# Eight fused transformer and Mamba batches on one core: stack reload in four transfers per table, LoRA rows on one partition, maxima over two key tiles, masks on diagonal columns

## What is computed

```python
x = _layernorm(x + _L0_attn_ref(x, ...), axis=-1)   # two causal attentions, 16 heads of width 8
x = _layernorm(x + _L0_ffn_ref(x, ...), axis=-1)    # FP4-quantized gated FFN, inner width 352
x = _layernorm(x + _L1_attn_ref(x, ...), axis=-1)   # Mamba block: 256 channels, 16 states, scan over time
x = _layernorm(x + _L1_ffn_ref(x, ...), axis=-1)    # FFN of width 512 with token-made low-rank weights
```

## Time and profile before

| | |
|---|---|
| runs, device us | 1017.21 median, 1008.09 to 1023.85 |
| profiled execution, device us | 1005.87 |
| its span, first to last instruction, us | 1003.6 |
| PE / VectorE / ScalarE / GpSimd busy | 692.3 / 724.7 / 461.2 / 153.4 us |
| mean granted TensorE clock | 0.849 of 2.4 GHz |
| DMA moved | 65.93 MB, 66 GB/s |

### The profile page before, as it was taken

One profiled execution on the slowest core, in us unless ns is written; L12 is line 12 of the kernel. 1 busy time (PEld: TensorE's weight loads), 2 busy tenths in 40 slices (PEclk: granted clock), 3 DMA queues, 4 the chain that ended last, 5 costly groups with the idle time before them and its releaser, 6 DMA issues.

```text
span 1003.6 us, 12436 instructions
## 1 busy us (share of the span) xinstructions
PE 692.3 (69%) x4131; PEld 407.2 (41%) x4131; DVE 724.7 (72%) x1295; ACT 461.2 (46%) x931; POOL 153.4 (15%) x265
## 2 busy tenths in 40 slices
PE   3247665786679776877778667956795777855555
PEld 1124344344544444434533454434543453433122
DVE  2716156986789687968897788868896779863951
ACT  2213432662566246634556356625662256436312
POOL 5512013013110412002300230022100000000000
PEclk9997867797889889889979897989898798976775
DMA  4421501361035303350136103520353013002300
GB/s 120 78 54 40 100 1 38 108 139 24 11 99 138 68 0 107 103 103 0 43 120 126 24 11 118 136 48 10 97 133 67 1 47 115 22 0 70 104 0 5
DMA packets 41151, 65.93 MB, mean 66 GB/s; under 512 B 8113, under 2 KB 30338, under 8 KB 38786
## 3 DMA queue, kind: packets, MB, share of 16 engines
q1 hardware_dynamic: 38946, 64.51, 26.0%
q10 hardware_dynamic: 2176, 1.05, 0.6%
HBM read 57.68 MB, written 7.86 MB: 65 GB/s over the span
## 4 chain that ended last, share of the span: by engine, by line
PE 37%; DVE 33%; DMA 11%; ACT 8%; issue 8%; SPq 1%; POOL 0%; DVEq 0%; ACTq 0%
PE ps_s L1052 9%; PE ps_f L1052 8%; DVE shared L1006 6%; PE ps_n L1052 6%; DMA bcrow<-bc_dram 6%; PE ps_y L1052 6%; PE ps_v L1052 6%; DMA x_tm<-in_L_attn_x_dram 5%; DVE mx L893 4%; DVE shared L1000 4%; DVE shared L1011 2%; ACT lmem L757 1%; DVE bn L814 1%; ACT L760 1%; ACT adisc L731 1%
## 5 line engine op out<-in xcount | busy, mean ns | idle before, releaser
L1052 PE MATMUL ps_y<-shared,ident 128*128 128x512 f32 x256 | 146.7, 702 | 52.3 <-DVE shared L1011 52.1
L1052 PE MATMUL ps_s<-stack_mem 72*128 72x128 bf16 (+2 forms) x1280 | 162.9, 248 | 4.8 <-DVE mx L893 4.4
L893 DVE TENSOR_REDUCE mx<-ps_s 128x4 f32<-128x512 f32 x192 | 126.6, 685 | 52.5 <-PE ps_s L1052 49.3
L1006 DVE TENSOR_TENSOR_SCAN shared<-adisc,shared 128x1024 f32<-128x1024 f32 x64 | 146.7, 2292 | 2.2
L1052 PEld LDWEIGHTS ps_s<-stack_mem 72*128 72x128 bf16 (+1 forms) x1280 | 111.1, 106 | 75.6 <-issue 32.0
L649 ACT ACTIVATE probs<-ps_s 128x512 f32<-128x512 f32 x192 | 105.5, 598 | 66.2 <-PE ps_s L1052 64.2
L731 ACT ACTIVATE adisc<-delta,amat 128x255 f32<-128x255 f32 x256 | 108.1, 504 | 39.0 <-DVE shared L1006 28.8
L1052 PE MATMUL ps_s<-causalT,ident_bf 128*128 128x512 bf16 x192 | 83.1, 433 | 23.1 <-DVE mparts L902 14.1
L1000 DVE TENSOR_TENSOR shared<-u,bcrow 128x1024 f32<-128x1024 f32 x64 | 78.0, 1218 | 28.0 <-DMA bcrow<-bc_dram 27.8
L1052 PEld LDWEIGHTS ps_y<-shared,ident 128*128 128x128 f32 x256 | 50.2, 218 | 107.6 <-DVE shared L1011 64.8
L1052 PE MATMUL ps_s<-causal,ident_bf 128*128 128x512 bf16 x128 | 55.3, 432 | 46.7 <-DVE mx L893 36.8
(11 more groups left out here) (213 smaller groups left out, 1114.2 us busy)
## 6 DMA issues: line engine op xcount, KB each, us to landing
bcrow<-bc_dram SPq DMA_DIRECT2D x64, 512.0 KB, 4.2
stack_mem<-stack_dram SPq DMA_DIRECT2D x48, 192.0 KB
stack_mem<-stack_dram SPq DMA_DIRECT2D x144, 64.0 KB
stack_dram<-parts SPq DMA_DIRECT2D x24, 256.0 KB, 2.3
x_tm<-in_L_attn_x_dram ACTq DMA_DIRECT2D x8, 128.0 KB, 11.4
xb<-in_L_attn_x_dram SPq DMA_DIRECT2D x8, 128.0 KB, 2.8
out_dram<-y_out SPq DMA_DIRECT2D x8, 128.0 KB, 2.5
fmem<-in_L_attn_conv_w_dram SPq DMA_DIRECT2D x1, 512.0 KB
```

Source lines behind the costliest of these rows:

```text
L893: V.tensor_reduce(mx[:, a, i, hd], ps_s[:, n % 2].rearrange("p (h n) -> p h n", n=P), AX.X, ALU.max).then_inc(s_max, 1)
L1006: V.tensor_tensor_scan(hs[:, j % HB].rearrange("p n c t -> p (n c t)"), adisc[:, j % 2].rearrange("p n c t -> p (n c t)"), bx[:, j % 2].re ...
L1052: return nc.tensor.matmul(o, lhsT, rhs, start=start, stop=stop, **kw)
```

## The change

1. **Stack reload.** The three repeats of each part are now read through a source with a repeated outermost dimension: one transfer of 72 rows (3 x 24) and three of 24 rows (3 x 8) per attention, 8 transfers a turn instead of 24. The semaphore counts follow.
2. **LoRA rows.** SP copies tokens 1 to 16 of `x3` into one partition (`lrow`). Eight matmuls with one contracted row make the outer products. `lorasel` and the selecting matmuls and copies are gone.
3. **Maxima.** Blocks are (0, 0) with four heads as before, and then query tile 1 against both key tiles with two heads each. `mx1` and its merge are gone.
4. **Masks.** They are added behind the scores, and only on the 128 diagonal columns of each head.
5. **Smaller edits.** PE adds `cstd` and `cgeo` in its transposing matmuls; relu and addition of `delta` are one instruction; `w2e` is one instruction instead of four; Gelu takes the bias directly; the table load at the start of each turn on ScalarE is gone.
6. **A new `PLAN`**, hence a new order on every engine.

```diff
@@ sp, prep @@
+                    sp.dma_start(stack[0:KROWS, 2 + a].rearrange("p h n -> p (h n)"),
+                                 stack_dram[2 + a].rearrange("i (d h) n -> (i d) (h n)", d=DH).unsqueeze(0).to_broadcast([3, 3 * DH, H * T])).then_inc(stack_r[a], 16)
                     for i in range(3):
                         rows = slice(i * 3 * DH, (i + 1) * 3 * DH)
-                        sp.dma_start(stack[rows, 2 + a].rearrange("p h n -> p (h n)"),
-                                     stack_dram[2 + a].rearrange("i (d h) n -> (i d) (h n)", d=DH)).then_inc(stack_r[a], 16)
-                        for j in range(3):
-                            rows = slice((3 * i + j) * DH, (3 * i + j + 1) * DH)
-                            sp.dma_start(stack[rows, a].rearrange("p h n -> p (h n)"),
-                                         stack_dram[a, i].rearrange("(d h) n -> d (h n)", d=DH)).then_inc(stack_r[a], 16)
+                        sp.dma_start(stack[rows, a].rearrange("p h n -> p (h n)"),
+                                     stack_dram[a, i].rearrange("(d h) n -> d (h n)", d=DH).unsqueeze(0).to_broadcast([3, DH, H * T])).then_inc(stack_r[a], 16)
@@ sp, lora_ffn @@
+                sp.wait_ge(x3_sb, b + 1)
+                sp.dma_start(lrow, x3[1:1 + 4 * LR, 0, :]).then_inc(lr_r, 16)
@@ vector, core, norm, mamba, lora_ffn @@
-                    V.tensor_reduce(mx[:, a, i, hd], ps_s[:, n % 2].rearrange("p (h n) -> p h n", n=P), AX.X, ALU.max).then_inc(s_max, 1)
+                    V.tensor_reduce(mx[:, a, min(i, 1), hd[0]:hd[-1] + 1:2], ps_s[:, n % 2].rearrange("p (h n) -> p h n", h=len(hd)), AX.X, ALU.max).then_inc(s_max, 1)
-                        V.tensor_tensor(mx1[:, a], mx[:, a, 1], mx[:, a, 2], ALU.max).then_inc(mx_sb, 1)
-                V.tensor_tensor(comb, cstd[:].rearrange("p t h d -> p t (h d)"), comb, ALU.add).then_inc(comb_sb, 1)
-                chain(V.tensor_scalar(drelu, dpre, 0.0, None, ALU.max))
-                V.tensor_tensor(delta[:], drelu, dexp, ALU.add).then_inc(delta_sb, 1)
+                V.scalar_tensor_tensor(delta[:].rearrange("p c t -> p (c t)"), dpre.rearrange("p c t -> p (c t)"), 0.0,
+                                       dexp.rearrange("p c t -> p (c t)"), ALU.max, ALU.add).then_inc(delta_sb, 1)
@@ tensor, core: score blocks @@
+                    else:
+                        for c, h in enumerate(hd[2 * i - 2:2 * i]):
+                            mm(bank[:, c * T:(c + 1) * T], stack[0:KROWS, a, h, P:T],
+                               stack[0:KROWS, 2 + a, h, :], start=(c == 0), stop=False)
+                        last = mm(bank.rearrange("p (h k n) -> p h k n", k=2, n=P)[:, :, 1], ident_bf[:],
+                                  causal[:].unsqueeze(1).to_broadcast([P, 2, P]), start=False)
@@ tensor, core: transposed blocks @@
-                        mm(ps_s[:, n % 3, :], ident_bf[:], causalT[:].unsqueeze(1).to_broadcast([P, 2, T]), stop=False)
+                        last = mm(ps_s[:, n % 3, :].rearrange("p (h q n) -> p h q n", q=2, n=P)[:, :, 0], ident_bf[:],
+                                  causalT[:].unsqueeze(1).to_broadcast([P, 2, P]), start=False)
@@ tensor, lora_ffn @@
+                    for p in range(LR):
+                        even, odd = (lrow[:, (2 * (LR * i + p) + k) * D:(2 * (LR * i + p) + k + 1) * D] for k in range(2))
+                        last = mm(ps_n[:, p * P:(p + 1) * P], odd, even)
@@ PLAN, two of its lines @@
-        "prep": [47.6, 47.6, 52.8, 55.1, 86.6, 105.3],
+        "prep": [38.5, 38.5, 42, 47.3, 87.6, 97.7],
```

More of the change, by code:

```diff
@@ L355, in build, with run @@
         ALL_ATT, ALL_W = 16 * len(attention_loads), 16 * len(loads)
[L357 removed]
+        def run(eng, chain, name, streams, setup=None):
             def turn(k):
@@ L488, in _ @@
             G.memset(wq_raw, 0.0).then_inc(s_pool0, 1)
-            for t_ in (lorasel, vz):
-                last = G.memset(t_[:], 0.0)
-            chain(last)
+            chain(G.memset(vz[:], 0.0))
             for s in range(2):
@@ L1219, in norm @@
                 yield
-                pe.wait_ge(comb_sb, f + 1)
+                pe.wait_ge(cstd_sb, f * 2 + 2)
                 for t in range(TT):
-                    last = tr(ps_n[:, t * P:(t + 1) * P], comb[:, t])
+                    for i, part in enumerate((cstd, cgeo)):
+                        last = mm(ps_n[:, t * P:(t + 1) * P], part[:, t].rearrange("p h d -> p (h d)"), ident[:], start=(i == 0), stop=(i == 1))
                 last.then_inc(combT_ps, 1)
```

185 lines of the change are left out of this document (78 added, 107 removed).

## The result

The changed kernel took 1012.25 us (1010.53 to 1013.83, 12 runs). The kernel before, run beside it, had a median of 1009.4 us over 12 runs that scatter from 992 to 1024. The ratio that leaves out its slow runs is 1.0131, 95% interval 1.0095 to 1.0167; a second series (1011.89 against 1011.69 us) gave 1.0045 (1.0013 to 1.0077). So by the ratios the change costs between a half and one and a half per cent, and by the medians 0.3% and nothing. By the ratios the sign of the forecast was right; its size (+53 us) was not, and the change lies within the 2% that the prediction called no change.

A forecast was written before the change was run, and what follows sets the result against it. The prediction took x_tm landing behind the reload's drain to bound the turn: 57.9 + 24.8 + 3.2 + 30.7 + 0.7 = 117.3 us against 107.6. 66.0 us late less 13 gave +53, so 1070 us, range 1000 to 1158.

The forecast's parts named there:

- The reload: Stack reload on the DMA engines: three engines, 96 rows each at 0.32 us, draining in 30.7 us a turn.
- x_tm lands when the reload has drained: x_tm's load waits behind the reload's rows; reload issue to next transposes 34.6 us, turns of 117.3 instead of 107.6 us.
- The rival that had x_tm pass the queue: Three engines, but TensorE waits only for the stack's first half: about 973 us; chance 0.06.
- 57.9 us from x_tm's transposes to the first scan step: First piece of the loop, TensorE's x_tm transposes to the first scan step, kept at 57.9 us from the kernel before.
- same columns: nothing: LoRA on TensorE: eight outer products replace nine selecting and two wide products, worth nothing.
- The bcrow load ahead of the reload, 6.1 us a turn: Last bcrow load issued before the reload on SP: VectorE's 6.1 us stall a turn goes.
- The start and the end: x_tm transposes: second at 71.9, third at 144.4, eighth at 730.9 us; behind that 13 us given back.
- The tail: After the eighth transposes: one bcrow stall (6.1), slow products (1.9) and three turns of 1.6 us give back 13.
- The small edits: VectorE saves 1.6 us a turn where no transfer sets the end, none in the loop; TensorE and ScalarE edits nothing.
- The LoRA row load: Small load hidden by VectorE's quantization of x1; uncovered it costs 2.8 us a turn.

The follow-up runs named there:

- c_lora: The LoRA part of the change alone added to b_act_xearly, in the order of the kernel before: 993.01 us, ratio 0.982.
- b_bcrow_first: The kernel before with one due time changed, so that SP issues the last bcrow load ahead of the reload's first half: 1031.37 us, ratio 1.0148.
- b_act_xearly: The fastest base: kernel before with new reload at its old place, last bcrow load on ScalarE's queue, x_tm issued mid-turn before: 964.24 us, ratio 0.9552.
- a_old_reload: The changed kernel with the old reload put back (12 transfers for each attention instead of 4), order and everything else as changed: 1041.38 us, ratio 1.0275.

## Why the prediction was right or wrong

**The reload: right.** Three engines, 0.309 to 0.317 us a row (taken: 0.32), in flight for 31 us (taken: 30.7), a share of 0.19. The stall for bcrow went, 27.8 to 0.3 us.

**"x_tm lands when the reload has drained": wrong for the new reload, and this carried the forecast.** The prediction saw a landing of 12.4 us and the end of the traffic in the same microsecond, which is so, and took one for the cause of the other. Two queues take turns on an engine; beside the new reload x_tm's pieces go one to a row, and it lands in 9.1 us, with 128 rows still to come. From the reload's issue to the next transposes it was 21.6 us, not 34.6. The rows of the kernel before could not decide it in that turn, where 110 rows started during the load, some 14 for each of eight engines, against 16 pieces of x_tm; its first load under a reload, with 29 rows behind it, could have. The rival that had x_tm pass the queue was the nearest and got 0.06; one piece for one row of 8 KB was a third reading that was not considered.

**"57.9 us from x_tm's transposes to the first scan step", carried over: wrong by 7 us a turn, in the other direction.** The prediction took the middle of the turn as fixed and the LoRA, mask and order edits as worth nothing. Measured it was 64.8. By the rows above, 6.8 us are lost ahead of the first FFN product, through the new order and the LoRA products in it; 2.0 come back from there to the Mamba input products, since LoRA no longer stands between; and 2.1 are lost again behind that, where these products run at the low clock. That LoRA's edit costs is shown in before's order (c_lora: 29 us on the fastest base, 17.5 of them given back by products that only keep TensorE busy); in the changed order the split is a reading. What the prediction called "same columns: nothing" counted TensorE's work and not its idle stretches. The idle wait for x_tm has a low clock behind it as well: the mask of the score block at 449.50 takes 0.63 us, the same product at 477.42 takes 0.38.

**The bcrow load ahead of the reload, 6.1 us a turn: only together with the new reload.** Alone it lost 15 to 19 us. The prediction priced its gain by the stall and put the later reload into the loop, which was right, but did not see that the stall had stood beside the same wait: in b_bcrow_first VectorE's 27.8 us are gone and TensorE's wait for x_tm is 56.2 us instead of 17.6.

**The start and the end.** Forecast for the second, third and eighth transposes: 71.9, 144.4 and 730.9; measured 54.03, 119.16 and 670.77. The tail, from the eighth transposes to the end, was to give back 13 us; it took 339.1 against 338.7. The first part of it is longer by the costs above, and only the last part, from the last batch's first scan step, is shorter (66.4 against 76.2 us). The LoRA part alone does this (c_lora 66.5, b_act_xearly 76.0 us).

**The small edits.** 1.6 us of VectorE a turn were expected to count where no transfer sets the end. On the fastest base score part and small edits together gave 8 us, a microsecond a turn, which is barely within the intervals. The LoRA row load, held to be hidden, is waited for 14.1 us in eight turns, 1.8 a turn (2.8 was named if it lay open).

The sum: the first batch's scan starts 5.0 us earlier (182.4 against 187.4), five turns are 3.95 us longer each (19.8), the last two together 1.3 us longer, the end 9.8 us shorter: -5.0 + 19.8 + 1.3 - 9.8 = +6.3 us of span, 1009.9 against 1003.6.

## What to carry to other kernels

When a load lands as a queue runs empty, work out its landing also from its own pieces times what stands beside them on an engine, and look for a turn in which the two readings differ, before calling it queued behind. An edit that removes work from an engine off the path has to be priced by the idle stretch it leaves: here what followed such a stretch on TensorE ran at half the clock, and twelve products without a reader gave back 17.5 of the 29 us that removing work had cost. Moving real work there was not tried. And a load whose source is ready early (x_tm) is to be issued as early as its buffer allows: this one edit was worth 17 us in the changed kernel (995.2 against 1011.9) and 43 where the reload was early too (964.2 against 1007.7).

## What the runs showed of the hardware

- Two queues that met on three DMA engines alternated one piece each: 48 pieces of 512 B between 54 rows of 8 KB in the six microseconds from 443. Beside the old reload it was less even: no piece for three microseconds, then 128 in five. bcrow (8 pieces of 4 KB an engine) took 8.6 us beside the same rows, and 15.1 in one queue with the old ones.
- Fewer engines were faster for a bystander: rows of 8 KB took 0.31 us when three engines wrote places 8 or 24 partitions apart, and 0.65 to 0.74 us (a_old_reload) with the old reload, where eight write neighbours. Whether the number of engines or the places make the difference, no run here shows.
- Behind 5.56 us without a product TensorE's granted clock was 0.50 in the next 3 us; behind 5.12 us it was 0.50 and six transposes took 1.54 us, behind 1.13 us it was 1.00 and they took 0.87. Twelve products in such a stretch shortened c_lora by 17.5 us.
